# Expert tables in turn order, round counts packed in TensorE registers, row-split down projection

## What is computed

```python
router_logits = x @ gate_w                                  # 256 x 64 experts
routing_weights, selected = jax.lax.top_k(router_logits, 8)
routing_weights = jax.nn.softmax(routing_weights, axis=-1)
hidden_sorted = jnp.repeat(x, 8, axis=0)[order]             # tokens sorted by expert
gate = ragged_dot(hidden_sorted, gate_proj_w, group_sizes)  # 512 -> 192
up   = ragged_dot(hidden_sorted, up_proj_w, group_sizes)    # 512 -> 192
down = ragged_dot(silu(gate) * up, down_proj_w, group_sizes)# 192 -> 512
out  = sum over the 8 experts of a token of down * routing_weight
```

## Time and profile before

| what | value |
|---|---|
| median of 3 runs | 379.88 us (377.63 to 380.1) |
| profiled execution, its own time | 380.15 us |
| its span | 378.4 us |
| TensorE matmuls, busy | 323.2 us (85%), 3092 |
| VectorE, busy | 166.6 us (44%) |
| ScalarE, busy | 119.3 us (32%) |
| GpSimd, busy | 85.3 us (23%), 376 |
| HBM read | 82.49 MB, mean 219 GB/s |
| gate/up matmuls L1109 | 896 records, 80.0 us busy |
| down matmuls L1131 | 672 records, 54.0 us busy |

### The profile page before, as it was taken

One profiled execution on the slowest core, in us unless ns is written; L12 is line 12 of the kernel. 1 busy time (PEld: TensorE's weight loads), 2 busy tenths in 40 slices (PEclk: granted clock), 3 DMA queues, 4 the chain that ended last, 5 costly groups with the idle time before them and its releaser, 6 DMA issues.

```text
span 378.4 us, 9715 instructions
## 1 busy us (share of the span) xinstructions
PE 323.2 (85%) x3092; PEld 184.3 (49%) x3093; DVE 166.6 (44%) x450; ACT 119.3 (32%) x190; POOL 85.3 (23%) x376
## 2 busy tenths in 40 slices
PE   0699999889967524998999999998999999999894
PEld 0554444447743413445555555554654555555462
DVE  7733565945856770133233333333333332333233
ACT  1112202154731401143334433343333433333431
POOL 4000003200000003222243224423342322422320
PEclk9999999995989655799999999999999999999999
DMA  2999959100000039002999805993993999999501
GB/s 60 357 403 408 408 188 377 40 3 0 2 2 0 0 113 388 1 0 76 363 356 382 325 0 185 396 390 112 381 381 153 337 383 392 394 387 396 205 0 55
DMA packets 39743, 83.22 MB, mean 220 GB/s; under 512 B 4648, under 2 KB 12976, under 8 KB 39600
## 3 DMA queue, kind: packets, MB, share of 16 engines
q1 hardware_dynamic: 39312, 82.99, 58.5%
q10 hardware_dynamic: 416, 0.04, 0.1%
HBM read 82.49 MB, written 0.52 MB: 219 GB/s over the span
## 4 chain that ended last, share of the span: by engine, by line
PE 53%; DVE 12%; POOLq 11%; issue 9%; POOL 8%; ACT 4%; DVEq 2%; ACTq 0%
PE psum L1076 12%; POOLq L489 7%; PE psum L1131 6%; PE psum L1109 6%; PE psum L906 4%; PE psum L945 4%; PE psum L918 4%; PE psum L1084 3%; POOL store L496 3%; POOL store L501 3%; POOLq L490 2%; DVE store L728 2%; PE psum L1118 2%; POOL store L505 2%; PE psum L1006 2%
## 5 line engine op out<-in xcount | busy, mean ns | idle before, releaser
L1109 PE MATMUL psum<-store 128*32 128x384 f32 x896 | 80.0, 499 | 0.7 <-ACT store L856 0.7
L1076 PE MATMUL psum<-store 128*128 128x128 bf16 x696 | 45.9, 222 | 18.6 <-DVE store L728 18.2
L1076 PEld LDWEIGHTS psum<-store 128*128 128x128 bf16 x696 | 40.9, 99 | 38.8 <-DVE store L728 25.6
L496 POOL TENSOR_TENSOR store<-store,slot_row 128x64 f32<-128x64 f32 x112 | 29.5, 295 | 123.4 <-issue 120.4
L1131 PE MATMUL psum<-store 128*32 128x256 f32 (+1 forms) x672 | 54.0, 454 | 0.0
L501 POOL TENSOR_TENSOR store<-store 128x64 f32<-128x64 bf16 x112 | 29.5, 295 | 96.5 <-PE psum L1118 95.9
L1109 PEld LDWEIGHTS psum<-store 128*32 128x32 f32 x896 | 29.2, 112 | 39.9 <-issue 34.7
L873 ACT ACTIVATE y_parts<-psum,w_slot 128x512 fp32r<-128x512 f32 x28 | 19.2, 687 | 77.7 <-PE psum L1131 77.7
L1084 PE MATMUL psum<-y_parts,place_T 128*128 128x512 f32 x120 | 36.0, 423 | 4.1 <-DVE y_parts L711 2.5
L868 ACT ACT_TABLE_LOAD x28 | 35.9, 1283 | 7.1 <-issue 6.9
L856 ACT ACTIVATE store<-psum 128x512 f32<-128x512 f32 x29 | 17.3, 598 | 61.2 <-PE psum L1076 61.2
(11 more groups left out here) (207 smaller groups left out, 357.6 us busy)
## 6 DMA issues: line engine op xcount, KB each, us to landing
store<-n_L_ffn_gate_proj_w_dram SPq DMA_DIRECT2D x64, 384.0 KB, 5.7
store<-in_L_ffn_up_proj_w_dram SPq DMA_DIRECT2D x64, 384.0 KB, 6.0
store<-n_L_ffn_down_proj_w_dram SPq DMA_DIRECT2D x64, 256.0 KB, 5.7
store<-n_L_ffn_down_proj_w_dram SPq DMA_DIRECT2D x64, 128.0 KB, 5.9
store<-in_L_attn_w_qkv_dram SPq DMA_DIRECT2D x1, 3072.0 KB, 14.4
store<-in_ctx_dram SPq DMA_DIRECT2D x2, 1024.0 KB, 6.3
store<-in_L_attn_w_out_dram SPq DMA_DIRECT2D x1, 1024.0 KB, 16.5
x_sb<-in_x_dram SPq DMA_DIRECT2D x1, 512.0 KB, 4.3
```

The costliest lines, as they stand in the source:

```text
L496: last = pool.tensor_tensor(apart[:, :, j], over_slots(rank, e), slots, ALU.subtract)
L1076: last = pe.matmul(bank[3][:, c * P:(c + 1) * P], xparts[:, h, part, c, :], pick_t[:, h], start=(k == 0), stop=(k == 3 * TH - 1))
L1109: last = pe.matmul(bank[0][quarter, 0:2 * INTER], xs[:, c, quarter], w[:, :, c, :], start=(c == 0), stop=(c == DC - 1))
```

## The change

- **Tables in turn order.** Ranks and router weights are transposed, multiplied with the turn table and copied back (`turned`), so that a team's four columns lie side by side. Teams 0 to 2 use the tables as they are. GpSimd does one operation for four experts in place of four, and a table `slot_no` over rounds replaces the moving of ranks. It reads no expert numbers.
- **Counts of rounds** are packed as base-8 digits in two integers (`packs`); TensorE loads both once, takes the lowest digit for a team and shifts. Its loop over 4 laps becomes two loops over 2 laps, so that there are eight bodies in place of four. The wait for the weights stands inside the round loop.
- **Down projection.** The tail of a down weight is loaded by two transfers, left half to partitions 0 to 63, right half to 64 to 127: five transfers per expert. `hid` is 256 wide without zeros, there are two transposes, and the down matmuls go in two halves of 256 columns to two PSUM banks, the tail over 64 rows each.
- **Before the loop.** Clears go to the head of VectorE's list or between its other steps; the split of the tokens in three parts goes to GpSimd; top-8 is done half by half; the first pick and gather use `pick_0`, made from the ranks; router weights come before the ranks; the matmuls that clear the output banks come before the ranks.
- **One Silu** of a single element on ScalarE ahead of the loop.

```diff
@@ weights of a team @@
-   (lane[:, TAIL_AT:SLOT_W], down_proj[bass.ds(e, 1), MAIN_I:].rearrange("e r (h n) -> (e r h) n", h=2))):
+   (lane[0:TAIL_I, TAIL_AT:SLOT_W], down_proj[bass.ds(e, 1), MAIN_I:, 0:D // 2].rearrange("e r n -> (e r) n")),
+   (lane[TAIL_I:, TAIL_AT:SLOT_W], down_proj[bass.ds(e, 1), MAIN_I:, D // 2:].rearrange("e r n -> (e r) n"))):
@@ GpSimd before the loop @@
+   pool.tensor_tensor(rest[:, h], xn[:, h].rearrange("p (q c) -> p c q", c=DC), xparts[:, h, 0], ALU.subtract)
+   pool.tensor_tensor(xparts[:, h, 2], rest[:, h], xparts[:, h, 1], ALU.subtract)
@@ GpSimd, one round @@
-   team = [pool.value_load(turns[0:1, bass.ds(q * TEAM + j, 1)], ...) for j in range(TEAM)]
-   for j, e in enumerate(team):
-       last = pool.tensor_tensor(apart[:, :, j], over_slots(rank, e), slots, ALU.subtract)
+   pool.tensor_tensor(apart, over_slots(table[:, 1]), slots, ALU.subtract).then_inc(s_ap, 1)
-   for j, e in enumerate(team):
-       last = pool.tensor_tensor(mix_t[:, :, j], pick_t[:, :, j], over_slots(rw, e), ALU.mult)
+   pool.tensor_tensor(mix_t, pick_t, over_slots(table[:, 0]), ALU.mult).then_inc(s_mx, 1)
-   for j, e in enumerate(team):
-       last = pool.tensor_tensor(left, left, blk_c[:, :, :], ALU.subtract)
@@ VectorE, head of its list @@
+   for q in range(TEAMS // 2):
+       ch.step(dve.memset(radix[:, q::TEAMS // 2], float(8 ** q)), wait=False)
+   dve.memset(place_T[:, :].bitcast(F32), 0.0).then_inc(s_mt, 1)
+   dve.memset(y_parts[:, :, :].bitcast(F32), 0.0).then_inc(s_yl, 1)
@@ VectorE, counts @@
+   ch.step(dve.scalar_tensor_tensor(spare[:, :], rounds[:, :], -1.0, radix[:, :], ALU.add, ALU.mult))
+   ch.step(dve.tensor_reduce(radix[:, 0:2], spare[:, :].rearrange("p (w q) -> p w q", w=2), AX.X, ALU.add))
+   dve.tensor_copy(packs[:, :], radix[:, 0:2]).then_inc(s_cnt, 1)
@@ ScalarE before the loop @@
+   act.activation(flipped[0:EXP_N], bank[7][0:EXP_N, :]..., ACT.Copy).then_inc(s_flc, 1)
+   act.activation(turned, bank[6][:, 0:4 * EXP_N]..., ACT.Copy).then_inc(s_tn, 1)
+   act.activation(warm[:, :], ntop[0:1, 0:1], ACT.Silu).then_inc(s_warm, 1)
@@ TensorE before the loop @@
+   pe.wait_ge(s_pk0, 1)
+   pe.wait_ge(s_trn, 1)
+   gather(pick_0)
+   (the two list matmuls, and four that bring the tables in turn order)
+   pe.wait_ge(s_cnt, 3)
+   word = [pe.value_load(packs[0:1, w:w + 1], ...) for w in range(2)]
@@ TensorE, one round @@
-   for k in range(3):
+   for k in range(2):
        last = pe.transpose(bank[1][:, k * P:(k + 1) * P], hid[:, k * P:(k + 1) * P], ident[:, :])
...
-   for k, (cols, at) in enumerate(((slice(0, D), DOWN_AT), (slice(0, D // 2), TAIL_AT), (slice(D // 2, D), TAIL_AT))):
-       for e in range(TEAM):
-           last = pe.matmul(bank[6][quarter, cols], hidT[:, k, quarter], ring[r][:, e, at:...], ...)
+   for k in range(2):
+       for half in range(2):
+           for e in range(TEAM):
+               rows = slice(0, P) if k == 0 else slice(half * TAIL_I, (half + 1) * TAIL_I)
+               at = TAIL_AT if k else DOWN_AT + half * (D // 2)
+               last = pe.matmul(y_half[half][quarter, :], hidT[rows, k, quarter],
+                                ring[r][rows, e, at:at + D // 2], start=(k == 0), stop=(k == 1))
@@ TensorE, counts @@
-   pe.wait_ge(s_w[r], 16 * 4 * TEAM * loads)
-   count = pe.value_load(rounds[0:1, bass.ds(q, 1)], min_val=1, max_val=TOK // BLK)
+   count = pe.snap((pe.snap(left) & 7) + 1, min_val=1, max_val=TOK // BLK)
+   (in the round loop) pe.wait_ge(s_w[r], 16 * 5 * TEAM * loads)
+   (after it) pe.reg_mov(left, pe.snap(left) >> 3)
```

More of the change, by code:

```diff
@@ new lines, in _, with gather @@
+            last.then_inc(s_num, 1)
+            for a, ready in ((0, s_rw), (1, s_rk)):
+                pe.wait_ge(ready, 1)
+                for h in range(TH):
+                    last = pe.transpose(bank[7][0:EXP_N, (a * TH + h) * P:(a * TH + h + 1) * P], rw_rank[:, a, h], ident[:, :])
+            last.then_inc(s_flp, 1)
+            def gather(chosen_slots):
+                for c in range(DC):
+                    for k, (part, h) in enumerate((part, h) for part in range(3) for h in range(TH)):
+                        last = pe.matmul(bank[3][:, c * P:(c + 1) * P],
+                                         xparts[:, h, part, c, :], chosen_slots[:, h], start=(k == 0), stop=(k == 3 * TH - 1))
+                last.then_inc(s_xg, 1)
@@ new lines, in _ @@
+            pe.wait_ge(s_xp, 2)
+            pe.wait_ge(s_pk0, 1)
+            pe.wait_ge(s_trn, 1)
+            gather(pick_0)
+            pe.matmul(bank[1][0:1, 0:EXP_N], col_i[0:EXP_N, :], turn[0:EXP_N], start=True, stop=True)
+            pe.matmul(bank[1][0:1, EXP_N:2 * EXP_N], size[0:EXP_N], turn[0:EXP_N], start=True, stop=True).then_inc(s_lst, 1)
+            pe.wait_ge(s_flc, 1)
+            for a in range(2):
+                for h in range(TH):
+                    at = (a * TH + h) * EXP_N
+                    last = pe.matmul(bank[6][:, at:at + EXP_N], flipped[0:EXP_N, a, h], turn[0:EXP_N], start=True, stop=True)
@@ L1096, in _ @@
+            last.then_inc(s_tnp, 1)
+            pe.wait_ge(s_cnt, 3)
+            word = [pe.value_load(packs[0:1, w:w + 1], min_val=0, max_val=8 ** (TEAMS // 2) - 1) for w in range(2)]
             step = pe.alloc_register("pe_step")
             pe.reg_mov(step, 0)
-            def team_rounds(q, r, loads):
-                pe.wait_ge(s_w[r], 16 * 4 * TEAM * loads)
-                count = pe.value_load(rounds[0:1, bass.ds(q, 1)], min_val=1, max_val=TOK // BLK)
+            left = pe.alloc_register("pe_counts_left")
```

212 lines of the change are left out of this document (108 added, 104 removed).

## The result

The changed kernel takes **373.64 us** (median of 20 runs, 367.17 to 377.36) against 376.9 us for the kernel before in the same comparison (20 runs, 372.3 to 380.1). Executions of either kernel fall into a faster and a slower group, and the ratios in this document compare the faster groups alone: here 0.985, with a 95% interval of 0.980 to 0.989, where the medians over all runs differ by 0.9%. I had forecast 355.0 us and a range up to 364; the direction was right and more than four fifths of the gain did not come. The profiled execution took 375.13 us with a span of 373.2.

A forecast was written before the change was run, and what follows sets the result against it. TensorE's rounds, with GpSimd waits at team changes, bound the kernel; weight reloads had 9 us slack. First gate/up 141.1, +1.3 clock, +128.1 rounds, +69.2 for late weights, +13.55 tail, +1.75 outside the span: 355.0 us, range 347 to 364.

The forecast's parts named there:

- Start +1.3: Kernel start: ten memsets at the head of VectorE's list cost 1.3 us (0.9 to 1.9).
- First gate/up at 141.1: Stage before the expert loop: 10.0 us saved, so with the later start the first gate/up comes at 141.1.
- First round +1.3 for the clock: First loop round: half clock adds 0 to 2.6 us over a full-speed round; the middle, 1.3, was taken.
- Down projection 1.52: Each round's down projection: 1.75 us, less 0.43 for overlapping row halves, plus 0.2 for mode switches, gives 1.52.
- Transposes -0.11: Hidden-state transposes in each round: two instead of three save 0.11 us.
- Team change 7.20: Round into a new team: GpSimd's wait goes, VectorE's load is late by 0.14 us, so 7.20 us.
- SyncE's period 13.7: Weight issuing for a late team: 11.65 us plus four more transfers at 0.52 each, 13.7 us.
- forecast wait of 4.6 us: Before the last team: weights arrive 4.6 us later than TensorE needs, giving back the gain of the last rounds.
- a wait in an earlier team than the last: Sign against the forecast: it is wrong if TensorE's wait for weights begins before the last team.
- rival C: Weight queue: 64-row transfers make the kernel slower, the load chain continuous above a 15.3 us period; 402 at 19; chance 0.05.
- Counts in registers 0: TensorE's round counts as packed words in registers: worth 0, since the load is hidden while the down projection streams.
- early Silu 0: One Silu ahead of the loop: worth 0, since ScalarE's table loads are covered by gate/up whether they go or stay.

The follow-up runs named there:

- four_tf: Changed kernel with the down tail in one transfer (rows misplaced), 64-row tails streamed before the 128-row pass and an earlier hidden-state wait: 352.5 us, ratio 0.940.
- wide5: Changed kernel with the old down projection, its main part loaded in two 256-column transfers, five 128-partition transfers an expert: 364.8 us, ratio 0.967.
- old_down_5: Changed kernel with the old down projection, its tail loaded in two contiguous transfers of 64 partitions: 377.3 us, ratio 1.006.
- half_tail: Changed kernel with the old down projection and two 64-partition tail transfers, the second left out from the fifth team on: 364.7 us, ratio 0.974.
- tail_first2: Changed kernel with its five transfers an expert, the 64-row tails streamed ahead of the 128-row pass: 374.9 us.
- old_down: Changed kernel with the down projection of before: tail in one 128-partition transfer, three transposes, matmuls over 128 rows: 363.0 us, ratio 0.957.
- dve_words: Changed kernel with the old down projection, VectorE taking its rounds per team from packed words in registers: 357.2 us, ratio 0.955.

## Why the prediction was wrong, step by step

**Start +1.3: right.** The first norm moved by 1.28 us, and moving two clears back takes the 1.28 away again.

**First gate/up at 141.1: measured 141.11, by luck.** From the first gating matmul to it the sum had 139.8 - 126.5 = 13.3 us, and the trace has 15.1 (126.02 to 141.11), 1.8 too many; the gating began 1.8 us earlier than the 127.8 of the sum, as in the execution before the clock was also at half from 111.2 to 114.7, and here it was not. Executions differ there by up to 6 us. "First round +1.3 for the clock": it was 9.84 us, because the whole gate/up ran at half clock; +1.5 against the sum.

**Down projection 1.52: measured 1.79.** Its two terms held together, the overlap of the row halves (16 weight loads in 0.18 us) and the switches, since `four_tf` gives 1.48; the size of each was not measured alone. What was missing: with the 64-row tails last, the first weight load of the next gate/up comes after 0.61 us of "issue". That TensorE's instruction stream has no lead left there is argued. Tails first with an earlier wait mends it; the two were not tried apart. **Transposes -0.11: right** (0.14 instead of 0.25). So a round is 7.36, not 7.06.

**Team change 7.20: measured 7.46 to 7.94.** GpSimd's wait is gone, as forecast. But what is late at a change is not VectorE's load, as I had it: the five intervals that hold only this load take 7.35 to 7.40 us, although on the old down projection it costs 0.37. The six that hold only TensorE's own change of team take 7.48 to 7.94, with up to 0.7 us of "issue" before the gate/up; with the old down projection the same six take 7.38 to 7.40. So the row-packed down projection also exposes TensorE's instructions at a change, which the sum had at nothing. With the slower rounds this is +8.5 us from the second gate/up to 330.79, the 24 intervals of which the sum makes 24 x 7.06 + 13 x 0.14 = 171.3 and the trace 179.8.

**SyncE's period 13.7: measured 15.0 to 16.1. This step failed, and it decided.** The sum priced four more transfers at 0.52; `wide5` shows that this is right for 128 partitions, and `old_down_5` and `half_tail` that those of 64 cost 0.47 each and slow the issue behind them. The forecast wait of 4.6 us before the last team became two, 4.8 and 5.9, each with a gate/up at half clock behind it; a wait in an earlier team than the last was one of the prediction's own signs of being wrong. The last two intervals are 12.08 and 15.32, 8.4 us over the sum, and the tail of the kernel 15.0 instead of 13.55. Together 1.5 + 8.5 + 8.4 + 1.5 = 19.9 of the 20.1 us between 355.0 and 375.1.

These terms are not independent. From the fourth team's end at 217.96 SyncE's chain is unbroken, eight teams to 341.24 and 17 us to the last gate/up. `tail_first2` had most of the 0.3 us a round and still ended at 373.4: the slow rounds cost nothing while the queue was slower. This is rival C's mechanism, which I had placed wrongly. I let its chain begin with team 4's load at 164.0, above a period of 15.3, and priced it at 1.4 us a new transfer. But the eighth team's load waits for the end of the fourth team, and the chain runs unbroken only from there. By the sum's own times that end comes at 142.4 + 10 x 7.06 + 3 x 0.14 = 213.4 and the eighth team's at 270.5, so, as an estimate, this chain governs at every period above (270.5 - 213.4) / 4 = 14.3, or at 0.66 us for each new transfer in place of 0.52. An expert's issuing grew by 0.83, and the engines lost a fifth of their rate.

The Trainium skill (DMA: Bandwidth & Descriptors, Measured) says, from transfers that GpSimd issued, to batch them to 1 MiB or more, and calls those under 64 KB descriptor-dominated. The traces agree in direction only: 313 GB/s with tails of 64 KB against 391 with tails of 128 KB, and none of an expert's transfers is above 384 KB.

**Counts in registers 0, early Silu 0, GpSimd no longer the bound: right**, the first two as measured on the old down projection. GpSimd's wide operations take 0.61 and 0.62 us each; where its "issue" wait was 2.92 us, the longest is now 0.79.

The gain of the joined stage and of the team changes is real: `old_down` has 207.0 us in the loop instead of 214.7, and 15.1 us from the first gating matmul to the first gate/up instead of 23.3. The transfers of the row-packed down projection took most of it back.

## What to carry to other kernels

Price a re-laid-out weight by its transfers as well as by its matmuls: saving 0.3 us a round on TensorE by splitting a transfer in two was a loss here, where the queue needed 12 us for a late team that TensorE used up in some 8, and lived on a lead of 9 us. Ask for each chain that ends just before the bound by how much its period may grow, and check both the issuing engine and the rate of the DMA engines, since removing one uncovers the other. When an engine's wait disappears, reprice the loads that had hidden under it on the neighbours.

## What the hardware showed that I had not expected

- A transfer onto 64 partitions is dearer to issue than one onto 128 with twice the bytes (0.47 against 0.33 us), and the engines move less with such transfers among the others: 329 GB/s at a share of 1.02, against 388 at 1.04.
- A 128-partition transfer whose source runs over halves first has two 4-byte packets where the others have 16, and holds up the next issue for 2.6 to 3.4 us: 216 GB/s with engines 0.63 busy.
- The time at which the expert loop starts depends on the clock in the attention stage. The clock rows of `dve_words`, first gate/up at 136.68, and of `old_down`, 143.13, with the same code up to there but for registers:

```profile
PEclk9999999999999855999999999999999999999998
```

```profile
PEclk9999999997799955899999999999999999999999
```

  Where slices 10 to 12 are granted in full, the first gating matmul comes at 121.4 to 121.7, otherwise at 124.0 to 128.0, and the loop starts about 15 us behind it in nearly every kernel of either kind. All kernels of the study show one or the other, so most of the spread inside one kernel's runs is probably this; what brings the dip on was not found.
